# A causal mask added on TensorE: from two half-contractions on 64x128 tiles to four 64x64 tiles

## The reference

```python
xn = _layernorm(x, axis=-1)
# attention
q, k, v = (to_heads(t) for t in jnp.split(xn @ w_in.T + b_in, 3, axis=-1))
scores = jnp.einsum('bhqd,bhkd->bhqk', q * scale, k)
causal_bias = jnp.where(jnp.tril(jnp.ones((slen, slen), dtype=bool)), 0.0, -jnp.inf)
attn = jax.nn.softmax(scores + causal_bias, axis=-1)
out = jnp.einsum('bhqk,bhkd->bhqd', attn, v)     # then heads joined, @ w_out.T + b_out
# experts: combine holds the two largest router weights of each token
g = silu(einsum('td,edf->etf', xn, w_gate)) * einsum('td,edf->etf', xn, w_up)
y = einsum('te,etd->td', combine, einsum('etf,efd->etd', g, w_down))
x = x + out + y + swiglu_mlp(xn, sw_gate, sw_up, sw_down)
```

## Time and profile before

| | us |
|---|---|
| median of 3 runs (633.5 to 633.7) | 633.7 |
| the profiled execution's own time | 633.35 |
| its span, first to last instruction | 631.6 |
| TensorE matmuls busy | 555.9 (88%) |
| VectorE busy | 467.0 (74%) |
| ScalarE busy | 346.7 (55%) |
| GpSimd busy | 349.7 (55%) |
| mask matmuls (line 473), 640 | 54.6 |
| products of the natural scores (line 482), 512 | 61.1 |
| one period of the loop, first gate product to the next one's (191.04 and 262.06 in the chain) | 71.0 |

### The profile page before, as it was taken

How to read it: one execution, slowest core, us unless ns; L and a number is a source line. 1 busy time by engine, 2 the same in 40 slices (tenths; PEclk the granted TensorE clock), 3 DMA queues, 4 the chain that set the end, 5 groups by cost and what they waited for, 6 DMA issues and landing times.

```text
span 631.6 us, 12497 instructions
## 1 busy us (share of the span) xinstructions
PE 555.9 (88%) x4144; PEld 312.8 (50%) x4144; DVE 467.0 (74%) x781; ACT 346.7 (55%) x472; POOL 349.7 (55%) x357
## 2 busy tenths in 40 slices
PE   1435999999999999999999999999999999999784
PEld 0223664466535664466535664466525664466422
DVE  3973997589785997589785997589785997489512
ACT  1511349733794349733794349733794349733591
POOL 3322763468354873468354873468354864468342
PEclk9857999999999999999999999999999999999897
DMA  5828103450137002550137002440137002540000
GB/s 143 268 94 193 38 5 105 144 142 18 36 121 205 28 20 104 139 144 17 38 117 197 37 20 103 141 142 17 38 119 210 23 20 103 151 135 18 7 2 17
DMA packets 43031, 57.10 MB, mean 90 GB/s; under 512 B 4529, under 2 KB 28433, under 8 KB 42833
## 3 DMA queue, kind: packets, MB, share of 16 engines
q1 hardware_dynamic: 43008, 56.83, 30.2%
HBM read 41.60 MB, written 15.20 MB: 90 GB/s over the span
## 4 chain that ended last, share of the span: by engine, by line
PE 62%; DVE 12%; DMA 8%; issue 7%; ACT 6%; SPq 4%; POOL 1%; POOLq 0%; DVEq 0%; ACTq 0%
PE banks L582 10%; PE banks L453 6%; PE banks L555 6%; PE banks L482 6%; PE banks L455 6%; PE banks L454 6%; ACT probs L772 5%; PE banks L464 5%; PE banks L473 4%; DVE neg_max L1080 4%; DMA q_op<-m_dram 3%; PE banks L466 3%; PE banks L465 3%; DMA cb<-c_dram 2%; DMA m_dram<-max_rows 2%
## 5 line engine op out<-in xcount | busy, mean ns | idle before, releaser
L1080 DVE TENSOR_REDUCE neg_max<-banks 128x2 f32<-128x1024 f32 (+3 forms) x224 | 194.7, 915 | 34.4 <-PE banks L473 33.5
L772 ACT ACTIVATE probs<-banks 128x1024 f32<-128x1024 f32 x160 | 154.2, 1032 | 12.9 <-PE banks L555 11.3
L835 POOL TENSOR_TENSOR probs<-probs,cb 128x512 f32<-128x512 f32 x88 | 116.0, 1318 | 76.2 <-ACT probs L724 73.1
L868 POOL TENSOR_SCALAR_AFFINE_SELECT probs<-probs 128x512 f32<-128x512 f32 x128 | 90.9, 731 | 107.3 <-ACT probs L772 107.0
L841 POOL TENSOR_TENSOR hid_lo<-probs,hid_hi 128x512 fp32r<-128x512 f32 (+1 forms) x88 | 113.1, 1285 | 66.9 <-ACT hid_hi L731 66.9
L724 ACT ACTIVATE probs<-banks 128x512 f32<-128x512 f32 (+1 forms) x112 | 67.0, 598 | 144.1 <-PE banks L455 142.9
L1062 DVE TENSOR_TENSOR probs<-probs,banks 128x512 f32<-128x512 f32 (+1 forms) x112 | 75.5, 680 | 33.5 <-PE banks L455 15.1
L453 PE MATMUL banks<-x_hi,w_hi 128*128 128x512 f32 (+1 forms) x224 | 94.4, 421 | 4.5 <-DVE w_lo L1215 2.7
L731 ACT ACTIVATE hid_hi<-probs 128x512 fp32r<-128x512 f32 (+1 forms) x112 | 70.3, 628 | 47.0 <-DVE probs L1062 46.0
L582 PE MATMUL banks<-probs,v_op 128*32 128x512 f32 (+3 forms) x1024 | 95.2, 444 | 0.4
L455 PE MATMUL banks<-x_hi,w_lo 128*128 128x512 f32 (+1 forms) x224 | 89.9, 401 | 0.0
(11 more groups left out here) (114 smaller groups left out, 604.2 us busy)
## 6 DMA issues: line engine op xcount, KB each, us to landing
cb<-c_dram SPq DMA_DIRECT2D x32, 256.0 KB, 4.5
q_op<-q_dram SPq DMA_DIRECT2D x32, 192.0 KB
k_op<-k_dram SPq DMA_DIRECT2D x32, 192.0 KB
cb<-c_dram SPq DMA_DIRECT2D x16, 224.0 KB, 4.6
q_dram<-q_parts SPq DMA_DIRECT2D x8, 384.0 KB, 2.5
k_dram<-k_parts SPq DMA_DIRECT2D x8, 384.0 KB, 2.5
cb<-c_dram SPq DMA_DIRECT2D x16, 192.0 KB, 4.4
cb<-c_dram SPq DMA_DIRECT2D x16, 160.0 KB, 4.5
```

Source lines behind the costliest of these rows:

```text
L772: nc.scalar.activation(probs[:, g % 2, 2 * u:2 * u + 2, :], ring[:, at:at + 2, :], ACT.Exp).then_inc(exp_done, 1)
L835: nc.gpsimd.tensor_tensor(sg[k % 3][:, :], sg[k % 3][:, :], cb[:, TILE_ORDER[k], :], ALU.mult).then_inc(weighted, 1)
L868: return nc.gpsimd.affine_select(out=view, in_=view, compare_op=ALU.is_ge, fill=0.0, base=0, pattern=[[0, 4], [1, P]], channel_multiplier=-1)
L1080: return nc.vector.tensor_reduce(out, in_, AX.X, ALU.max, negate=True)
```

## The change

The mask is added by four matmuls on 64x64 quarters of the array. Weights are the 64x64 identity on both partition halves; `c` says which half of the queries, and so of the array's columns and of PSUM's partitions, a matmul serves. The first half of the queries (c = 0) streams all 128 columns of a block, the second (c = 1) only the last 64, because none of its first 64 keys is masked. Each part needs one contraction of 64 only. The products stay as they are. Mask and identity are loaded and cast in the smaller shapes; the four loads remain four.

```diff
-        ident_half = sb("ident_half", [P, 2, P], BF16)
-        mask_half = sb("mask_half", [P, 2, P], BF16)
+        ident_half = sb("ident_half", [P, HALF], BF16)
+        mask_half = sb("mask_half", [P, P], BF16)
...
-                     (mask_f[0:HALF, :, :], causal.rearrange("(a p) n -> p a n", p=HALF)),
-                     (mask_f[HALF:P, :, :], causal.rearrange("(a p) n -> p a n", p=HALF)),
-                     (ident_f[0:HALF, :, :], ident.rearrange("(a p) n -> p a n", p=HALF)),
-                     (ident_f[HALF:P, :, :], ident.rearrange("(a p) n -> p a n", p=HALF)),
+                     (mask_f[0:HALF, :], causal[0:HALF, :]),
+                     (mask_f[HALF:P, :], causal[0:HALF, :]),
+                     (ident_f[0:HALF, :], ident[0:HALF, 0:HALF]),
+                     (ident_f[HALF:P, :], ident[0:HALF, 0:HALF]),
...
-            def mask_scores(bank, a, at, stride, nblk, last):
-
-                blocks = bank[:, a, :].rearrange("p (k n) -> p k n", n=stride)[:, :, at % stride:at % stride + P]
+            def mask_scores(bank, a, c, at, stride, nblk):
+
                 own = slice(HALF * a, HALF * (a + 1))
-                mm = pe.matmul(blocks[:, at // stride:at // stride + nblk, :], ident_half[own, last, :],
-                               mask_half[own, last, :].unsqueeze(1).to_broadcast([HALF, nblk, P]),
-                               start=False, stop=(last == 1), skip_group_check=True)
-                return mm
+                cols = slice(at % stride + HALF * c, at % stride + P)
+                blocks = bank[HALF * c:HALF * (c + 1), a, :].rearrange("p (k n) -> p k n", n=stride)
+                return pe.matmul(blocks[:, at // stride:at // stride + nblk, cols], ident_half[own, :],
+                                 mask_half[own, 0:P - HALF * c].unsqueeze(1).to_broadcast([HALF, nblk, P - HALF * c]),
+                                 start=False, stop=True, tile_position=(HALF * a, HALF * c), skip_group_check=True)
...
-                for last in range(2):
+                for c in range(2):
                     for a in range(2):
-                        mm = mask_scores(bank, a, *masks, last)
+                        mm = mask_scores(bank, a, c, *masks)
                 mm.then_inc(nat_ready, 1)
...
-            nc.vector.tensor_copy(ident_half[:, :, :], ident_f[:, :, :]).then_inc(const_made, 1)
-            nc.vector.tensor_copy(mask_half[:, :, :], mask_f[:, :, :]).then_inc(const_made, 1)
+            nc.vector.tensor_copy(ident_half[:, :], ident_f[:, :]).then_inc(const_made, 1)
+            nc.vector.tensor_copy(mask_half[:, :], mask_f[:, :]).then_inc(const_made, 1)
```

More of the change, by code:

```diff
@@ L161, in block_kernel @@
         after = 2 * FT + NT * E
-        mask_f = early[:, after:after + 2 * P].rearrange("p (a n) -> p a n", a=2)
-        ident_f = early[:, after + 2 * P:after + 4 * P].rearrange("p (a n) -> p a n", a=2)
+        mask_f = early[:, after:after + P]
+        ident_f = early[:, after + P:after + P + HALF]
         att = probs[:, 0, 0, :].rearrange("p (q e) -> p q e", q=QT)
```

## The result

The changed kernel took 644.15 us (median of four runs, 641.40 to 649.36) beside 633.7 us for the kernel before: 1.0174 times as long, 95% interval 1.0126 to 1.0221. Run again beside the kernel before it took 643.04 us beside 632.88: 1.0163 (1.0126 to 1.0199). So the times differ by some 10.3 us. The profiled execution is one of 645.37 us.

What follows compares the result with a forecast made beforehand. TensorE was taken to bound the expert stage; tile changes and loads less saved streams add 1.43 us a batch, 11.4 for eight, less 0.4 for loads: +11.0, giving 644.7 us, range 638 to 655.

Steps and rivals of the forecast that it cites:

- What binds: Expert stage from the fifth score pair on: TensorE bounds, busy 25.00 of 25.00 us; VectorE, at 24.09, has almost no room.
- fourth rival: VectorE bounds after all and longer masks only fill short TensorE gaps: 633 to 637 us, chance 0.06.
- The change of tile: Each switch between the products' 64x128 tile and the mask's 64x64 quarters costs TensorE 0.095 us, bounds 0 and 0.10.
- third rival: No pause between the two tiles of 64 rows, so the kernel gets faster: 626.9 us, bounds 622 and 631, chance 0.11.
- point of decision: From slot 4 on, the cost per tile change under which the kernel gets faster: 0.034 us.
- Streams: A mask's four quarter matmuls run together, one stream per block instead of two, saving 0.10 us (256 columns) or 0.05 (128).
- The size of a pair: Added time per score pair: +0.02 us with 256 mask columns, +0.07 with 128, +0.105 on top for a slot's second pair.
- way back: Tile change from a mask to the next pair's products, 7 times a batch in slots 4 to 10: +0.105 us with load.
- The two signs named ahead: Expected in the changed profile: mask block to next products' start about 0.24 us wide and 0.19 narrow, in mid-slot.
- the weight load: Loading the quarters' 64-column mask weights after a tile change: near 110 ns, 0.025 us exposed, bounds 0.01 and 0.10.
- The first part: Slots 1 to 3: three exposed wide pairs add 0.06 us, pair 0 adds 0.035, pair 1 hides in a 0.7 us wait.
- The prologue: Ahead of the loop, the four mask and identity loads become plain blocks and issue faster: 0.4 us saved, between 0 and 0.9.

Runs made afterwards that it cites:

- two-column matmul: Kernel before plus one two-column matmul of zeros per pair ahead of the mask: 665.81 us on a 64x64 quarter, 635.39 us on the 64x128 tile.
- kernel grouped by slot: Changed kernel, but where a slot has two pairs in a row, both pairs' products come first, then both masks: 638.75 us, 1.0086 to the kernel before.
- compact kernel: Kernel before, tile kept, whole mask with each contraction half streaming 64 columns and one weight row carrying the fully masked half block: 626.00 us, 0.9897.

## Why the prediction was right

**What binds.** Right: TensorE, with VectorE close behind. TensorE stays at 25.00 of 25 us, VectorE's waits grow, and a mask half as long takes 1.05 us off the stage before VectorE is full. The fourth rival would have left the stage where it was; it grew by 1.13 us.

**The change of tile.** Predicted 0.095 us, with 64x128 to 64x64 not in the trace. In the trace from start to start it is 0.09 us more for each of the three lengths of product ahead of a mask (0.316 us instead of 0.222 behind 512 columns). The two-column matmul gives 0.10, its load included, by another way. So the third rival, no pause between tiles of the same 64 rows, is out: its point of decision was 0.034 us.

**Streams.** Right: four quarters at once, and the saved columns worth 0.8 us a batch where no tile changes.

**The size of a pair.** Here the sum was too large. Slot 5 with two wide pairs and one way back grew by 1.10 - 0.99 = 0.11 us, not 2 x 0.02 + 0.105 = 0.145. Slot 4 with two narrow ones went from 207.19 to 207.96 = 0.77 us to 210.09 to 211.07 = 0.98: +0.21, not 2 x 0.07 + 0.105 = 0.245. The seven slots from 4 to 10 of that batch add up from 6.22 to 7.36 us: +1.14, not 3 x 0.145 + 2 x 0.245 + 2 x 0.195 = 1.315, so 0.025 less a slot. With 0.10 for the way back a wide pair costs +0.01 and a narrow one +0.06, each 0.01 less than predicted, and slots from 4 on add 9 x 0.01 + 6 x 0.06 + 7 x 0.10 = 1.15 us instead of 1.335. The two signs named ahead show the same: a block of 0.23 and 0.17 us, not 0.24 and 0.19. The term is the weight load with the streams together. The load is recorded at 103 ns, against a guess near 110:

```profile
L474 PEld LDWEIGHTS banks<-mask_half,ident_half 64*64 64x64 bf16 x640 | 18.1, 103 | 35.1 <-issue 35.1
```

By the prediction's own rule, 85 ns of it latency, 0.018 us lie open instead of 0.025, which is 0.007 of the 0.01; the rest is less than starts of 0.01 us can show. No run splits load and streams.

The prediction also put what the matmuls between the pairs gain or lose at nothing. From slot 4's first pair to the last pair 22.30 us (207.19 to 229.49) become 23.33 (210.09 to 233.42), +1.03 and not the +1.14 of the pairs: the experts' matmuls between them took 0.1 us less. Why stays open. The first part grew by 0.10 us (12.09 to 12.19), as predicted.

**The prologue.** Predicted 0.4 us saved, measured nothing: the first pair's products start at 53.32 us, before at 53.27. The chain of the changed kernel shows the four issues (start us, us):

```profile
4.30 0.60 SPq L313
...
4.95 0.59 SPq L313
...
5.58 0.60 SPq L313
...
6.21 0.60 SPq L313
```

They take 0.6 us, near the 0.61 and 0.77 of the earlier trace rows, and not the 0.43 that the prediction read from a load of another shape: 0.2 us in all. TensorE's first matmul still came earlier, its waits for weights being 12.5 us instead of 13.5:

```profile
PE banks L404 <- DMA wo_sb<-in_woT: 12.5, 1, 12.5
...
PE banks L482 <- DMA k_op<-k_dram: 7.6, 1, 7.6
```

but the wait for the keys on their way through DRAM took 7.6 us instead of 6.1, and the lead was gone. Over all the runs that first pair starts between 51.7 and 53.4 us, with no order by the loads (52.16 in the kernel grouped by slot, which has the changed kernel's); a term of 0.4 us can't be seen in it. Whether the earlier start caused the longer wait stays open.

**The sum.** 11.4 - 0.4 = 11.0 us were forecast. The stage says 8 x 1.13 = 9.0 us, so the batch was put 8 x (1.43 - 1.13) = 2.4 us too high, and the 0.4 us of the prologue didn't come. The two comparisons gave 10.45 and 10.16 us; what they have above the stage is not located: the first profile has the half clock and a longer wait for DRAM, the second neither. That the total, 644.15 against 644.7, came so much closer than the stage is luck.

## What to carry to other kernels

Count the changes of tile, not the columns: a mask matmul of 0.1 us can't pay for a pause of 0.1 us on the way in and another on the way out, unless one visit serves more work, and waits that the new order brings can eat that gain too. Ask first whether the same columns can be saved on the tile in use; here that was worth 1% and put two engines in balance. A stage in which a second engine is 4% from full gives back part of every saving, so price the second engine's next wait before the first engine's gain.

## What the hardware did that was not expected

**The clock falls in the steady loop.** Ahead of the 3.4 us at 0.51 in the changed kernel's profile TensorE had waited 0.72 us for queries from DRAM, at 315.97, and ran for some 1.5 us after it; a matmul of 512 columns that took 0.50 us at 316.29 took 0.79 at 317.51. In the last batch, whose wait is longer, the clock falls in all twelve profiles, 0.02 to 1.7 us after it: in the kernel before the wait of 2.64 us ended at 595.66 and the fall came at 596.23, and over the runs these waits last 1.9 to 2.9 us. The other seven batches wait 0.27 to 0.72 us, and of all these waits only the one before 315.97 was followed by a fall; the 0.71 us before 462.12 in the same profile was not. No run here settles what decides.

**A pause in either direction, whichever side of the tile changes.** 64x128 to 64x64 (columns alone), 64x128 to 128x128 (rows alone) and 64x128 to 128x32 (both) all show 0.09 to 0.10 us; the way from 64x64 back to 64x128 lies in the 0.23 us block above.

**A copy that waits out another engine.** The predicated copy's 1.76 us without a mask are the 1.18 us that GpSimd's multiply still had to run and 0.58 us behind it. In the compact kernel the copy starts first, at 218.65, 0.03 us ahead of the multiply: it takes 0.73 us, and the multiply 1.82 us instead of about 1.28. The Trainium skill (SBUF — State Buffer, Who interferes with whom) has a pair of ports that VectorE and GpSimd share as a lock, held by whichever starts first while the other blocks, and puts a VectorE instruction with two inputs from SBUF among those that need it. These two rows agree with it, except that the one that waited then took 0.58 and 1.12 us more, each some 0.15 short of its usual time.
